# Two scaled fp16 parts for q and k, both attention passes on halves of the array's rows, and first-pass matmuls issued ahead of the second-pass one

## The reference

```python
q = shape((xn @ Wq + bq) * 16**-0.5); k = shape(xn @ Wk + bk); v = shape(xn @ Wv + bv)
attn = einsum('btd,bsd->bts', q, k)
attn = attn + _rel_to_abs(einsum('btd,md->btm', q, rel_k[0]))    # 9 relative keys, |s - t| <= 4
probs = softmax(attn); out = einsum('bts,bsd->btd', probs, v)
out = out + einsum('btm,md->btd', _abs_to_rel(probs), rel_v[0])
```

## Time and profile before

| | before |
|---|---|
| median of 3 runs (lowest, highest) | 2044.13 us (2041.16, 2046.0) |
| the profiled execution: its own time | 2041.84 us |
| its span, first to last instruction | 2039.7 us |
| busy: PE, PEld, DVE, ACT, POOL | 1782.0, 1023.4, 1479.1, 1099.6, 749.8 us |
| mean granted PE clock | 0.944 of 2.4 GHz |
| norm_and_project and route | to 196 us |
| group 0's first pass and windows | 196 to 286 us |
| groups 0 to 15 of the attention | 286 to 1144 us |
| experts and combine | 1144 to 2040 us |

### The profile page before, as it was taken

The page is one execution under the profiler, slowest core; times in us unless marked ns, Lnnn a source line. Parts: engine busy times, 40 slices in busy tenths (PEclk is TensorE's granted clock), DMA queues, the critical chain, the costliest instruction groups (busy, mean ns, idle before and its releaser), DMA issues. The chain is left out here.

```text
span 2039.7 us, 36131 instructions
## 1 busy us (share of the span) xinstructions
PE 1782.0 (87%) x11121; PEld 1023.4 (50%) x11121; DVE 1479.1 (73%) x2619; ACT 1099.6 (54%) x2115; POOL 749.8 (37%) x529
## 2 busy tenths in 40 slices
PE   6993359999999899999888599999999999999991
PEld 4772013333333233333222277777777777788881
DVE  3675687777777677777653298888888888888552
ACT  2552016767676566666878554444444454455550
POOL 1001574444444424475300044454354444443110
PEclk9896569999999999999999799999999999999996
DMA  5998764784444424657751477677677677676655
GB/s 177 330 349 265 243 191 119 210 229 122 113 123 118 121 83 124 209 143 213 237 184 43 169 233 231 216 231 236 213 222 244 205 223 244 215 224 190 195 149 173
DMA packets 227567, 395.56 MB, mean 194 GB/s; under 512 B 15440, under 2 KB 161760, under 8 KB 219296
## 3 DMA queue, kind: packets, MB, share of 16 engines
q1 hardware_dynamic: 193088, 279.97, 45.1%
q0 software_dynamic: 25824, 93.73, 15.0%
q10 hardware_dynamic: 8576, 20.97, 2.9%
HBM read 306.37 MB, written 87.99 MB: 193 GB/s over the span
## 5 line engine op out<-in xcount | busy, mean ns | idle before, releaser
L763 DVE CUSTOM_DVE_ANT_0 t_seen<-t_s,hide 128x1024 bf16<-128x1024 f32 x512 | 603.6, 1221 | 226.8 <-PE t_s L643 225.4
L828 ACT ACTIVATE t_pr<-t_s 128x512 f32<-128x512 f32 x1024 | 558.1, 605 | 250.3 <-PE t_s L656 163.9
L643 PE MATMUL t_s<-t_k,t_q 96*128 96x512 bf16 x1024 | 323.6, 399 | 78.7 <-DVE t_mx L763 54.6
L652 PE MATMUL t_s<-t_q,t_k 98*128 98x512 bf16 x1024 | 359.1, 387 | 35.3 <-ACT t_pr L828 23.9
L1373 ACT ACTIVATE e_sg<-e_pa,e_down 128x256 f32<-128x256 f32 x312 | 147.7, 473 | 424.7 <-PE e_pa L1248 420.6
L1444 DVE SCALAR_TENSOR_TENSOR e_wl<-e_ws,e_up,e_wh 128x512 f16<-128x512 f32 x312 | 318.8, 1034 | 13.5 <-ACT e_wh L1334 0.5
L1257 PE MATMUL e_py<-e_w2s,e_hT 128*128 128x256 f32 x1248 | 324.3, 383 | 0.0
L569 POOL TENSOR_TENSOR t_kw<-t_kw,t_qw 128x2304 f32<-128x2304 f32 x32 | 162.1, 5067 | 337.1 <-issue 307.0
L1248 PE MATMUL e_pa<-e_xh,e_wh 128*128 128x256 f16 x1248 | 239.8, 274 | 48.9 <-DVE e_xl L1436 41.8
L652 PEld LDWEIGHTS t_s<-t_q,t_k 98*128 98x128 bf16 x1024 | 96.9, 97 | 367.8 <-ACT t_pr L828 264.4
L667 PE MATMUL t_po<-t_pr,t_vx 128*32 128x512 f32 x2048 | 274.0, 607 | 0.7 <-ACT t_pr L828 0.7
(11 more groups left out here) (203 smaller groups left out, 1825.1 us busy)
## 6 DMA issues: line engine op xcount, KB each, us to landing
e_ws<-in_L_ffn_w_dram SPq DMA_DIRECT2D x78, 1024.0 KB, 5.0
e_w2s<-in_L_ffn_w_dram SPq DMA_DIRECT2D x39, 1024.0 KB, 6.1
e_vs<-v_rows POOLq DMA_DIRECT2D x32, 1152.0 KB, 5.9
t_kw<-k_rows POOLq DMA_DIRECT2D x22, 1152.0 KB, 10.3
t_q<-q_stack SPq DMA_DIRECT2D x32, 768.0 KB, 6.6
t_k<-k_stack SPq DMA_DIRECT2D x32, 768.0 KB, 10.8
t_kw<-in_L_ffn_w_dram ACTq DMA_DIRECT2D x16, 1024.0 KB, 5.0
t_kw<-k_rows SPq DMA_DIRECT2D x10, 1152.0 KB, 5.6
```

The source lines that it names most:

```text
L643: last = nc.tensor.matmul(s1[:, buf, half * CH:(half + 1) * CH], q1[0:ROWS, u, h, i * P:(i + 1) * P], k1[0:ROWS, u, h, half * CH:(half + 1 ...
L652: last = nc.tensor.matmul(s2[:, bank, :], k2[0:ROWS + MROWS, u, h, i * P:(i + 1) * P], q2[0:ROWS + MROWS, u, h, half * CH:(half + 1) * CH] ...
L763: nc.vector.tensor_tensor_reduce(out=seen[:, buf, :], in0=s1[:, buf, :], in1=c["hide"][:, (TB - 1 - i) * P:(TB - 1 - i) * P + L], scale=1. ...
L828: nc.scalar.activation(pr[:, k % BP, n % HG], s2[:, turn(u, n)], ACT.Exp).then_inc(exp_ok, 1)
```

## The change

- q and k are scaled by powers worked out at run time and cut into **two fp16 parts** in place of three bf16 ones. A stack has 3 x 16 = 48 rows in place of 96. DRAM holds each part once, and the attention loads each of its three slices by a DMA of its own, 16 partitions each.
- The scales come from bounds of q and k, made once: ACT squares Wq, Wk, the relative keys and the biases, PE sums the squares (5 small matmuls), DVE and ACT make the bounds and a tile `size` in 12 small operations. PE waits for it before Wv of chunk 0.
- The exponential takes off the scale by an operand from SBUF, `scale=size[:, 3:4]`.
- **Pass 1 lies on rows 0 to 47 of the array, pass 2 on rows 64 to 113** (`tile_position`); one tile holds both stacks. Of the mask, whose identity has 128 rows, two pieces of 64 rows each are needed, on rows 64 to 127: per group 72 short matmuls in place of 40, of 72, 68 or 4 columns in place of 136, 132 or 4.
- **Order:** the unit of pass 1 is now half a tile (one matmul), the halves due are issued **in front of** the second-pass matmul of their step.

```diff
+PARTS = 2
+Q_PARTS = (0, 0, 1)
+K_PARTS = (1, 0, 0)
+ROWS = len(Q_PARTS) * D
+SIDE = P // 2
+STACK = SIDE + MROWS
...
-        part = [sb(f"part{i}", [P, 2 * KC, CH], BF16) for i in range(3)]
+        part = [sb(f"part{i}", [P, 2 * KC, CH], F16) for i in range(PARTS)]
...
                     sp.dma_start(bcol[:, i, :], src.rearrange("(k p) -> p k", p=P),
                                  allow_slow_non_contiguous=True).then_inc(w_in, 16)
+                    sp.dma_start(brow[:, i, :], src.rearrange("(o e) -> o e", o=1).broadcast_to([P, E])).then_inc(w_in, 16)
...
-                    nc.vector.tensor_tensor(rest[:], qkT[:], part[0][:], ALU.subtract).then_inc(rest_ok, 1)
+                    for a in range(2):
+                        rows = slice(a * KC, (a + 1) * KC)
+                        last = nc.vector.scalar_tensor_tensor(out=part[1][:, rows, :], in0=qkT[:, rows, :], scalar=size[:, a:a + 1],
+                                                              in1=part[0][:, rows, :], op0=ALU.mult, op1=ALU.subtract)
+                    last.then_inc(part_ok[1], 1)
                     relative(n)
-                    nc.vector.tensor_tensor(part[2][:], rest[:], part[1][:], ALU.subtract).then_inc(part_ok[2], 1)
...
+                for a in range(2):
+                    nc.scalar.activation(wsq[:, a], w["qk"[a]][:], ACT.Square)
...
+                for a in range(2):
+                    for k in range(KC):
+                        nc.tensor.matmul(pv[:, 0, a * E:(a + 1) * E], full[:], wsq[:, a, k, :], start=(k == 0), stop=(k == KC - 1))
...
                 def load1(g, u):
-                    for dst, src in ((q1, sq), (k1, sk)):
-                        sp.dma_start(dst[0:ROWS, u], src[g]).then_inc(in1[u], 16)
+                    for dst, src, parts in ((qs, sq, Q_PARTS), (ks, sk, K_PARTS)):
+                        for j, part in enumerate(parts):
+                            sp.dma_start(dst[j * D:(j + 1) * D, u], src[g, part]).then_inc(in1[u], 16)
...
+                    n, half = n // 2, n % 2
                     h, i, buf = n // TB, n % TB, n % B1
...
+                    last = nc.tensor.matmul(s1[:, buf, half * CH:(half + 1) * CH], qs[lows, u, h, i * P:(i + 1) * P],
+                                            ks[lows, u, h, half * CH:(half + 1) * CH], start=True, stop=True, tile_position=(0, 0))
...
+                    last = nc.tensor.matmul(s2[:, bank, :], ks[highs, u, h, i * P:(i + 1) * P],
+                                            qs[highs, u, h, half * CH:(half + 1) * CH],
+                                            start=True, stop=not far, tile_position=(SIDE, 0))
+                    for x, (r, a, m, j) in enumerate(far):
+                        last = nc.tensor.matmul(s2[:, bank, a:a + m], c["eye"][SIDE:P, r, :], c["far"][SIDE:P, r, j:j + m],
+                                                start=False, stop=(x == len(far) - 1), tile_position=(SIDE, 0))
...
                     for n in range(XS):
-                        pass2(g, u, n)
-                        while more and done < min(X1, -(-X1 * (n + 1) // QUOTA)):
+                        while more and done < min(XS, -(-XS * (n + 1) // QUOTA)):
                             pass1(g + 1, 1 - u, done)
                             done += 1
+                        pass2(g, u, n)
...
-                        nc.scalar.activation(pr[:, k % BP, n % HG], s2[:, turn(u, n)], ACT.Exp).then_inc(exp_ok, 1)
+                        nc.scalar.activation(pr[:, k % BP, n % HG], s2[:, turn(u, n)], ACT.Exp,
+                                             scale=size[:, 3:4]).then_inc(exp_ok, 1)
...
+                for r in range(2):
+                    eye, far, low = c["eye"][:, r, :], c["far"][:, r, :], (1 - r) * SIDE
```

More of the change, by code:

```diff
@@ L99, in norm_and_project @@
         qkT = sb("qkT", [P, 2 * KC, CH])
[L100 removed]
+        brow = sb("brow", [P, 2, E])
+        wsq = sb("wsq", [P, 2, KC, E])
+        rsq = sb("rsq", [P, NM])
+        full = sb("full", [P, P])
+        bound = sb("bound", [P, 2, E])
+        most = sb("most", [P, 4])
         logits = sb("logits", [P, NT, X])
[L102 removed]
+        part = [sb(f"part{i}", [P, 2 * KC, CH], F16) for i in range(PARTS)]
         vrow = sb("vrow", [P, CT, E])
@@ L196, in _ @@
                 sp.wait_ge(st_rows, 32 * NC)
-                for p in range(3):
+                for p in range(PARTS):
                     sp.wait_ge(st_part[p], 16 * 2 * KC * NC)
@@ L201, in _ @@
             def _(pool):
+                nc.gpsimd.memset(full[:], 1.0).then_inc(full_ok, 1)
                 nc.gpsimd.memset(zpad[:], 0.0).then_inc(const_ok, 1)
@@ L320, in chunk @@
                     after(act, st_part[0], 16 * 2 * KC * n)
-                    nc.scalar.copy(part[0][:], qkT[:]).then_inc(part_ok[0], 1)
+                    act.wait_ge(size_ok, SIZES)
+                    for a in range(2):
+                        rows = slice(a * KC, (a + 1) * KC)
+                        last = nc.scalar.activation(part[0][:, rows, :], qkT[:, rows, :], ACT.Copy, scale=size[:, a:a + 1])
+                    last.then_inc(part_ok[0], 1)
                     if more:
@@ L394, in _ @@
                 pe.wait_ge(w_in, 16 * N_LOAD)
+                pe.wait_ge(full_ok, 1)
+                pe.wait_ge(square_ok, 1)
+                for a in range(2):
+                    for k in range(KC):
+                        nc.tensor.matmul(pv[:, 0, a * E:(a + 1) * E], full[:], wsq[:, a, k, :], start=(k == 0), stop=(k == KC - 1))
+                nc.tensor.matmul(pv[:, 1, 0:NM], full[:], rsq[:], start=True, stop=True).then_inc(norm_ok, 1)
                 pe.wait_ge(const_ok, 7)
@@ L651, in pass2 @@
                     far = far_pieces(i, half)
-                    last = nc.tensor.matmul(s2[:, bank, :], k2[0:ROWS + MROWS, u, h, i * P:(i + 1) * P],
-                                            q2[0:ROWS + MROWS, u, h, half * CH:(half + 1) * CH],
-                                            start=True, stop=not far)
-                    for a, m, j in far:
-                        last = nc.tensor.matmul(s2[:, bank, a:a + m], c["ident16"][:], c["far"][:, j:j + m],
-                                                start=False, stop=True)
+                    last = nc.tensor.matmul(s2[:, bank, :], ks[highs, u, h, i * P:(i + 1) * P],
[4 more added lines that the diff above has]
+                                                start=False, stop=(x == len(far) - 1), tile_position=(SIDE, 0))
                     last.then_inc(s2_ok, 1)
@@ L710, in _ @@
                 pe.wait_ge(ones_ok, 2)
-                pe.wait_ge(in1[0], 32)
-                for n in range(X1):
+                pe.wait_ge(in1[0], 16 * N_STACK)
+                for n in range(XS):
                     pass1(0, 0, n)
```

167 lines of the change are left out of this document (99 added, 68 removed).

## The result

| | before | changed |
|---|---|---|
| median of the runs, us (20 each, side by side) | 2041.7 (2038.7 to 2046.0) | 2048.3 (2040.7 to 2071.5) |
| ratio, 95% interval | | 1.004 (1.0026 to 1.0055) |
| profiled execution, us (span) | 2041.84 (2039.7) | 2044.16 (2042.4) |
| mean granted TensorE clock | 0.944 | 0.922 |

2022 was forecast. The kernel became slower, by little more than a measurement of it can tell. The execution of 2071.5 us counts as a slow one and is not in the ratio; the other 19 scatter over 26 us where those of before scatter over 7. What follows compares the two profiled executions, 2.7 us apart in span; the changed one lies 4 us under its median.

A forecast was written before the change was run, and what follows sets the result against it. PE was taken as the nearest bound of a group (48.5 of 51.94 us), DVE close; -23.9 + 0 + 2.8 + 2.1 - 3 = -22.0 us from 2044.1 gave 2022 us, own range 2004 to 2040, with rivals 1996 to 2062.

The forecast's parts named there:

- Overlap of the passes: Attention groups: a first-pass half tile and the second-pass matmul run side by side, the pair taking 0.22 us, not 0.43.
- no overlap: Rival, chance 0.15: in the groups the two passes do not run side by side; +2.5 us per group, 2082 us.
- incomplete: Rival, chance 0.12: the passes overlap only partly, pair 0.32 us; +0.8 us per group, 2056 us.
- the exponential is no dearer: Rival, chance 0.12: reading the scale from SBUF costs nothing; end wait 1.0 us shorter, group 15 by 2.8; 2006 us.
- The period of a full group: DVE sets the pace in groups 0 to 12: 50.1 us each, 1.84 less than before, -23.9 us in all.
- end wait: DVE's wait at the end of each group, after its 32 tiles: from 7.1 to 6.7 us.
- those inside: DVE's waits within the 52 steps of a group that carry tiles: 4.2 us, 5.6 before.
- Before the attention: Start of the kernel: scale work adds, smaller written parts count nothing, up to 5 us gain as bound; together +2.1 us.
- Group 0's first pass: Window and stack loads, 196 to 286 us: halved stack bytes against narrower loads; -3 us taken.
- Groups 13 and 14: Groups carrying ACT's weight sums: each between -1.8 and +5.6 us, 0 taken.
- Group 15: Group without a first pass: dearer exponentials cost between 0 and 5.6 us, +2.8 taken.
- The clock: Rival, chance 0.03: PE's idle time drops its clock to 1.2 GHz in the groups; about +250 us, 2290 us.

The follow-up runs named there:

- e12: Changed kernel with each part of q and k written three times, as many bytes as before; 2056.7 us beside 2041.0 for the kernel before, one execution.
- e15: Kernel before with the exponential's scale read from SBUF (a column of ones); 2100.2 us, ratio 1.007 to the kernel before.
- e2: Changed kernel plus an unread 512-column matmul on rows 0 to 47 in front of each second-pass matmul of group 15; 2086.8 us, ratio 0.999 to before.
- e13: e9 plus an unread matmul on rows 0 to 63 in front of each second-pass matmul of group 15; 2071.5 us, ratio 0.993 to the kernel before.
- e1: Changed kernel with the exponential's scale a constant in the instruction, not read from SBUF; 2090.4 us, ratio 1.002 to the kernel before.
- e9: Changed kernel with both passes padded to 64 rows, the added rows zero; 2029.0 us, ratio 0.993 to the kernel before.
- e14: e13 with 8 of the 16 weight sums moved to VectorE; 2063.2 us, ratio 0.992 to the kernel before.
- e16: Changed kernel padded to 64 rows, first-pass half behind the second-pass matmul as before; 2082.1 us, ratio 0.997 to the kernel before.
- e3: Changed kernel with the first-pass half issued behind the second-pass matmul, as before; 2092.0 us, ratio 1.003 to the kernel before.
- e6: Changed kernel with the order of before, plus unread matmuls in the last 8 steps of each group and all of group 15; 2051.8 us, ratio 1.006 to before.
- e7: e6 with 8 of the 16 weight sums moved to VectorE; 2052.3 us, ratio 1.006 to the kernel before.
- e10: e6 with both passes padded to 64 rows; 2045.0 us, ratio 1.003 to the kernel before.
- e11: e7 with both passes padded to 64 rows; 2043.2 us, ratio 1.002 to the kernel before.

## Why the prediction was wrong, point by point

- **Overlap of the passes: right.** 0.22 for the pair was taken; starts are 0.01 apart. Of the rivals "no overlap" and "incomplete" are out, and so is "the exponential is no dearer".
- **The period of a full group: right.** 50.1 forecast, 50.55 at the full clock, and in the padded kernel -21.0 of the -22.1 for groups 1 to 12. The exponentials are 0.58 apart (0.58). DVE's waits are 11.2 and 11.5 in groups 2 and 3 (10.9), of which the end wait is 5.9 (6.7) and those inside some 5.5 (4.2): two misses of about 1 us that offset each other. PE's waits for DVE are 18 us a group, not 10.
- **Before the attention: wrong by 12 us.** "PE is as full as the DMAs, so I count nothing, and up to 5 us of gain as a bound." PE's 96.6% hid that the DMAs at 1.01 held it: with the bytes cut PE went to 99.05% at a clock of 1.00, and e12 puts 10.5 us back. The bound itself was too small.
- **Group 0's first pass:** -4.2 for -3.
- **Groups 13 and 14:** 0 taken from -1.8 to +5.6 each; +9.0 for both, within the bounds. The operand is half of it or more (4.6 to 6.8, e15). The rest, 2 to 4 us, is put down to the low clock (45 us of it for 7), which no run tested by itself.
- **Group 15:** +2.8 taken; +18.9. The operand alone is +5.5 (e15), the upper bound; the clock is the other 13 to 14 (e2, e13). The two are not independent: without the operand half of the low-clock time goes too (e1).
- **The clock: the step that failed.** It had a chance of 0.03, against it that "34.7 of 50 is nearer to the busy stretch than to the idle one". That judged the clock by PE's busy time and asked only whether all of it falls. The change also halves the rows that each matmul works on, which the rows of before can't show, as the matmuls of both passes there stood on 96 and 98. And it came in part: in places, where PE also waits. It takes 13.6 us in groups 1 to 12 (e9; the order may have a share), 13 to 14 in group 15, 2 to 4 in groups 13 and 14: some 30 us. By this sum the change would have given some -27 without them, more than forecast, thanks to the start. No run reached that: the best, e14, is 0.8% or 17 us faster than before, with the zeros to set.

The misses add up to +24.7: start -11.9, first pass and group 0 -1.4, groups 1 to 12 +14.7, 13 and 14 +9.0, group 15 +16.1, experts -1.8. With the forecast of -22.0 that is +2.7, the difference of the spans. The median stands another 4 us higher; the dips fall differently in each trace, which may be why.

## What to carry to other kernels

Before halving the rows of a matmul, or packing two onto the array, look where it will stand alone or wait: there its clock may go, and the busy share did not tell of it here. Padding a contraction from 48 and 50 to 64 rows of zeros cost nothing in time per matmul here and brought the clock back in the full groups; matmuls on the free rows that nobody reads made group 15 shorter, though put into every group they came with new stops. Both are worth a run together with the packing. Where the DMAs' share is at 1, count a cut of their bytes as a gain though another engine looks just as full, and give a per-channel scale from SBUF its price (here 0.09 us for 128x512) wherever ScalarE sets the pace.

## What the runs showed that was not expected

- The granted clock follows the rows in use. Same columns, same order, groups 1 to 7: 96 and 98 rows 1.00, 66 rows 1.00, 48 and 50 rows 0.51 with PE busy all the time. Rows of zeros count (e9, e13, e14, e16). With 66 rows the matmul is also no longer on a half of the array, which these runs don't separate.
- On two of the four chips groups 11 and 12 take 64 to 69 and 81 to 87 us, in either kernel (e1 to e3, e13 to e16), while POOL scatters rows; the engines stand idle there for a remote event or for nothing that the profile shows (DVE 13.9 us in five waits in e13, 891 to 955 us). What this is stays open.
- A stop of PE at the start of a group costs more than itself. In e6, e7, e10 and e11 stops of 4.2 to 4.9 us make a group 6 to 9 us longer, with 3.4 to 13.7 us at 1.2 GHz in it. It is not a matter of the halves: in group 8 of the kernel before, on 96 and 98 rows, a stop of 5.9 us costs 9 us, with 10.2 at 1.2 GHz.
